# The first rest of each step moved from VectorE to GpSimd in a two-layer recurrence

## The reference

```python
def layer(x, h0, Wx, Wh, b):            # 8 x 1024 x 512, all f32
    xW = einsum('ntd,dh->nth', x, Wx) + b
    def step(h_prev, xw_t):
        h_next = tanh(h_prev @ Wh + xw_t)
        return h_next, h_next
    return scan(step, h0, xW over t)
x = x + layer(x, cond, L0_Wx, L0_Wh, L0_b)
x = x + layer(x, cond, L1_Wx, L1_Wh, L1_b)
```

## Time and profile before

| | us |
|---|---|
| median of 3 runs | 2107.1 (2107.07 to 2107.55) |
| the profiled execution | 2108.6 |
| span from first to last instruction | 2106.8 |
| TensorE busy | 2073.6 |
| VectorE busy | 1720.0 |
| ScalarE busy | 1121.5 |
| GpSimd busy | 14.2 |

### The profile page before, as it was taken

One profiled execution on the slowest core, in us unless ns is written; L12 is line 12 of the kernel. 1 busy time (PEld: TensorE's weight loads), 2 busy tenths in 40 slices (PEclk: granted clock), 3 DMA queues, 4 the chain that ended last, 5 costly groups with the idle time before them and its releaser, 6 DMA issues.

```text
span 2106.8 us, 213809 instructions
## 1 busy us (share of the span) xinstructions
PE 2073.6 (98%) x98432; PEld 1802.2 (86%) x98432; DVE 1720.0 (82%) x10233; ACT 1121.5 (53%) x4609; POOL 14.2 (1%) x15
## 2 busy tenths in 40 slices
PE   7899999999999999999999999999999999999997
PEld 5788888888888888888888888888888888888886
DVE  3788888888888888888888888888888888888886
ACT  2455555555555555555555555555555555555553
POOL 2000000000000000000000000000000000000000
PEclk9999999999999999999999999999999999999999
DMA  3000000000000000000000000000000000000000
GB/s 102 25 23 27 25 25 26 24 27 23 27 23 27 25 24 27 23 27 23 27 24 25 25 24 27 23 27 23 27 24 25 26 24 27 23 27 23 27 25 15
DMA packets 112075, 56.20 MB, mean 27 GB/s; under 512 B 12448, under 2 KB 111024, under 8 KB 111536
## 3 DMA queue, kind: packets, MB, share of 16 engines
q1 hardware_dynamic: 111456, 53.53, 8.9%
q10 hardware_dynamic: 432, 1.18, 0.2%
q0 software_dynamic: 32, 0.02, 0.0%
HBM read 37.90 MB, written 16.78 MB: 26 GB/s over the span
## 4 chain that ended last, share of the span: by engine, by line
PE 98%; issue 1%; DVE 0%; DMA 0%; ACT 0%; SPq 0%; ACTq 0%; DVEq 0%
PE ps_rec L225 43%; PE ps_rec L238 33%; PE ps_xw L206 21%; DMA wx<-wx_in 0%; DVE zt L370 0%; DVE z L376 0%; ACT h L305 0%; SPq L177 0%; SPq L175 0%; ACT ps_rec L300 0%; DVE x_out L420 0%; DVEq L369 0%; ACTq L304 0%; ACTq L299 0%
## 5 line engine op out<-in xcount | busy, mean ns | idle before, releaser
L225 PE MATMUL ps_rec<-wh,h 128*32 128x128 f32 x32896 | 1265.1, 273 | 16.8 <-ACT h L305 12.3
L238 PE MATMUL ps_rec<-wh_part,h 128*32 128x128 bf16 x48960 | 1062.5, 221 | 9.0 <-issue 8.9
L305 ACT ACTIVATE h<-z 128x32 f32<-128x32 f32 x2048 | 470.5, 230 | 846.3 <-DVE z L376 829.5
L225 PEld LDWEIGHTS ps_rec<-wh,h 128*32 128x32 f32 x32896 | 830.3, 109 | 102.6 <-ACT h L305 17.9
L238 PEld LDWEIGHTS ps_rec<-wh_part,h 128*32 128x32 bf16 x48960 | 713.9, 96 | 193.0 <-issue 10.7
L384 DVE TENSOR_TENSOR h<-h 128x16 f32<-128x16 f32 x4080 | 627.2, 154 | 303.0 <-ACT h L305 302.6
L300 ACT ACTIVATE ps_rec<-ps_xw,mask 128x128 f32<-128x128 f32 x2048 | 670.7, 328 | 123.1 <-PE ps_xw L206 97.2
L370 DVE STREAM_TRANSPOSE zt<-ps_rec 128x128 f32<-128x128 f32 x2048 | 638.0, 311 | 39.5 <-PE ps_rec L238 22.3
L376 DVE TENSOR_REDUCE z<-zt 128x32 f32<-128x96 f32 x2048 | 545.9, 267 | 1.5 <-DVE zt L370 0.9
L206 PE MATMUL ps_xw<-wx,x_pe 128*32 128x128 f32 x8192 | 403.1, 273 | 3.3 <-DMA wx<-wx_in 2.4
L206 PE MATMUL ps_xw<-wx,x_mid 128*32 128x128 f32 x8192 | 401.9, 273 | 0.0
(11 more groups left out here) (14 smaller groups left out, 13.5 us busy)
## 6 DMA issues: line engine op xcount, KB each, us to landing
x_pe<-x_t SPq DMA_DIRECT2D x256, 64.0 KB, 1.9
x_dve<-x_t SPq DMA_DIRECT2D x256, 64.0 KB, 2.0
out_t<-x_out SPq DMA_DIRECT2D x256, 64.0 KB, 1.5
wx<-wx_in SPq DMA_DIRECT2D x4, 256.0 KB, 8.2
wh<-wh_in ACTq DMA_DIRECT2D x1, 1024.0 KB, 8.3
wh<-wh_in SPq DMA_DIRECT2D x1, 1024.0 KB, 4.8
wx<-wx_in SPq DMA_DIRECT2D x1, 1024.0 KB, 8.2
bias<-b_in ACTq DMA_DIRECT2D x2, 64.0 KB, 3.3
```

Of the source, the lines that this page charges most:

```text
L225: mm = pe.matmul(rows(bank, g), h_step(l, n - 1)[:, k, :], wh[l][:, k, g * P:(g + 1) * P], start=False, stop=k == KC - 1 and whole.start = ...
L238: mm = pe.matmul(rows(bank, g), h_bits(l, n - 1)[:, k, :], wh_part[l][:, i, at:at + P], start=False, stop=k == whole.start - 1 and i == PA ...
L305: act.activation(h_of(l, n), z[l][n % 2][:, :].rearrange("p (k b) -> p k b", k=KC), ACT.Tanh).then_inc(h_last if (l, n) == (0, T - 1) else ...
```

## The change

`rest` becomes a function of the engine. The first rest of every split step is issued by GpSimd, one after another in the order of the steps, each after the same wait for tanh that VectorE had, and counts up `rest_done` as before. VectorE's list loses its two `rest_first`; its `rest_second` keeps its place and its wait. The rests of layer 1's starting state stay on VectorE. The renaming of a local variable (`rest` to `left`) changes nothing.

```diff
+        def rest(eng, l, n, part):
+
+            step, to, of, tiles = h_step(l, n), h_cols(n, part), h_cols(n, part - 1), slice(0, KB[l])
+            return eng.tensor_tensor(step[:, tiles, to], step[:, tiles, of], h_bits(l, n)[:, tiles, of], ALU.subtract)
...
+            for l, n in ORDER:
+                if is_split(l, n):
+                    pool.wait_ge(*h_count(l, n))
+                    rest(pool, l, n, 1).then_inc(rest_done[l], 1)
...
-            def rest_first(l, n):
-                if is_split(l, n):
-                    dve.wait_ge(*h_count(l, n))
-                    rest(l, n, 1).then_inc(rest_done[l], 1)
-
             def rest_second(l, n):
                 if is_split(l, n):
                     dve.wait_ge(rest_done[l], n + 1 if l else n + 2 - PARTED)
-                    rest(l, n, 2).then_inc(split_count(l, n)[0], 1)
+                    rest(dve, l, n, 2).then_inc(split_count(l, n)[0], 1)
...
                 sums(s)
-                if n0 is not None:
-                    rest_first(0, n0)
                 if n1 is not None:
                     turn(1, n1)
...
                     total(1, n1)
-                    rest_first(1, n1)
```

More of the change, by code:

```diff
@@ L358, in _ @@
                 pool.wait_ge(s_wh[l], DMA)
-                full, rest = wh[l][:, 0:KB[l], :].rearrange("p k d -> p (k d)"), wh_rest[l][:, :]
-                pool.tensor_tensor(rest, full, upper(full), ALU.subtract).then_inc(s_wrest[l], 1)
+                full, left = wh[l][:, 0:KB[l], :].rearrange("p k d -> p (k d)"), wh_rest[l][:, :]
+                pool.tensor_tensor(left, full, upper(full), ALU.subtract).then_inc(s_wrest[l], 1)
                 pool.tensor_copy(wh_part[l][:, 0, :], upper(full)).then_inc(s_wpart[l], 1)
                 pool.wait_ge(s_wrest[l], 1)
-                pool.tensor_copy(wh_part[l][:, 1, :], upper(rest)).then_inc(s_wpart[l], 1)
-                pool.tensor_tensor(wh_part[l][:, 2, :], rest, upper(rest), ALU.subtract).then_inc(s_wpart[l], 1)
+                pool.tensor_copy(wh_part[l][:, 1, :], upper(left)).then_inc(s_wpart[l], 1)
+                pool.tensor_tensor(wh_part[l][:, 2, :], left, upper(left), ALU.subtract).then_inc(s_wpart[l], 1)
+            for l, n in ORDER:
+                if is_split(l, n):
+                    pool.wait_ge(*h_count(l, n))
+                    rest(pool, l, n, 1).then_inc(rest_done[l], 1)
         @block.vector
@@ L466, in _ @@
             dve.wait_ge(s_hinit, 2)
-            rest(1, -1, 1).then_inc(s_hrest, 1)
+            rest(dve, 1, -1, 1).then_inc(s_hrest, 1)
             dve.wait_ge(s_hrest, 1)
-            rest(1, -1, 2).then_inc(s_hsplit, 1)
+            rest(dve, 1, -1, 2).then_inc(s_hsplit, 1)
             for s in range(T + LAG + 1):
```

## The result

The changed kernel takes 2112.3 us (median of 7 runs, 2109.7 to 2114.7) against 2107.1 (also 7 runs, 2105.4 to 2109.0): the ratio is 1.0024, 95% interval 1.0013 to 1.0035. It is slower by 5 us, a little more than the 0.2% that the prediction called the least that can be told. The time lies in the range that was given, but the forecast was "no change", and there is one. The profiled execution took 2111.05 us, its span 2109.3.

A forecast was written before the change was run, and what follows sets the result against it. The prediction took the ring through TensorE to hold half slots at 1.00 us. From 2108.6 us profiled, -1 us for half slots and +0.6 for the last eight steps gave 2108.2, median 2106.7; range 2100 to 2130.

The forecast's parts named there:

- What bounds the kernel: Opening step: two equal rings hold each half slot (one step) at 1.00 us, TensorE's floor just below at 0.99.
- The two rings of 1.00 us: Per half slot: one over VectorE and ScalarE (transpose, reduce, tanh, first rest), one through TensorE; each sums to 1.00 us.
- the floor of 0.99: TensorE's own minimum per half slot; about 0.01 us of each is TensorE waiting for the second rest, counted as busy.
- the ring through TensorE: Transpose, other layer's second rest, L238's split matmuls, next transpose: 1.00 us per half slot, read as the ring that holds.
- Does the transpose stand behind the first rest: Step on VectorE's queue: hold of 0 to 0.01 us per half slot, gain 0 to 20 us, taken as 1 us.
- The first rival: The first rest truly holds the transpose; half slots fall to 0.99, gaining 20 us, 2087 us; chance 0.10.
- GpSimd's cost: First rest on GpSimd: record taken as 0.20 us, between 0.10 and 0.26; waking after tanh 0.04 to 0.08 us.
- The room: From tanh's end to the second rest's start, 0.36 to 0.37 us; less two wakings, 0.25 to 0.29 for GpSimd's record.
- the second rival: GpSimd's record or waking exceeds the cover, deciding from 0.29 us; at 0.32, +41 us, 2147 us; chance 0.15.
- The sign that was named for it: If GpSimd decides: VectorE idle before its second rest, released by GpSimd, and L238's loads show idle time VectorE ends.
- the move at +0.07 in these steps: Last eight steps, layer 1 alone: tanh to second rest grows from 0.23 to 0.28-0.32 us, +0.6 us in all.
- The third rival: GpSimd twice as slow as VectorE, record 0.35 us: half slot 1.05, +102 us, 2208 us; chance 0.05.

The follow-up runs named there:

- The last experiment but one: Changed kernel without first rests, TensorE not waiting for the second rest, which goes to an unread tile: 2085.3 us, ratio 0.9915 to the kernel before.
- the first: Changed kernel with no first rest on any engine, the second rest waiting for tanh itself: 2105.2 us, ratio 0.9994 to the kernel before.
- the second measurement: Changed kernel as it is, measured again on one chip with its last three variants: 2111.5 us against 2103.9 for the kernel before, ratio 1.0039.

## Why the prediction was right or wrong

**What bounds the kernel: right.** The two rings of 1.00 us and the floor of 0.99 under them were read from the rows. The last experiment but one found the floor (19 us, forecast 18 and up to 2 more), and the first showed that the ring through TensorE is enough to hold 1.00 alone.

**Does the transpose stand behind the first rest: right.** The transposes are free in the changed kernel, 494 us of idle time ahead of them, and nothing was gained; without any first rest the gain is 0.0006 of the time, with an interval that includes none. What decided it in the rows was the reduce: the record of a transpose that is queued starts later, but what follows comes at 0.34 in place of 0.35 (in the changed kernel 0.35 again, 1000.58 to 1000.93). The first rival, 20 us, is out.

**GpSimd's cost: the record right, the waking at the edge.** I took 0.20 for the record, and it is 0.212. That is partly luck, as 0.20 was no more than a value picked between 0.10 and 0.26. One row was also misread on the way: the two memsets of 1,096 elements overlap, and each lasts 1.03 us, not half of 1.98. I took 0.04 to 0.08 for the waking, and it is 0.08 (1000.46 to 1000.54). The slow end of my own bounds was the true one.

**The room: this step failed.** The prediction took the room from tanh's end (1001.73) to the start of the second rest's record (1002.10) and subtracted two wakings, which left 0.25 to 0.29 us for GpSimd's record. The start of a record isn't the moment at which its input must be there. A second rest that stands behind a transpose has a record of 0.13, one whose input comes last has one of 0.18 (2095.36 above); both end at the same time if the late one starts 0.04 to 0.05 earlier. The cover is shorter by that: 0.25 less 0.05 is 0.20 us, and GpSimd takes 0.21. In the ring of the second rival, (1.71 + y) / 2, the 1.71 held the short record and the quick waking. With 0.05 and 0.04 added and y = 0.21 it is 2.01 / 2 = 1.005 in place of 0.96. The rival was the right mechanism with its deciding point at y = 0.29 in place of about 0.20, and so it was given 0.15 where it should have been the likeliest. The sign that was named for it, VectorE idle before its second rest and released by GpSimd, would have missed it too: that is 6.0 us in the whole changed kernel.

The number was within reach. The last steps of the kernel before show this very ring bare, with both rests on VectorE. After the tanh at 2093.12 and the reduce at 2094.77 of the earlier trace rows, the timeline of the kernel before goes on with the next tanh, 1.95 after the last:

```profile
2095.07 0.23 ACT L305 ACTIVATE h<-z 128x32 f32<-128x32 f32 x1 [1.49 <-DVE z L376]
```

The prediction itself put the move at +0.07 in these steps, and wrote it down as 0.6 us for eight of them. 1.95 + 0.07 is 2.02, over the 2.00 of two half slots: the same sum, applied to the middle, says slower by up to 0.01 for each half slot, 20 us at most. Measured, the step at the end went from 1.95 to 2.00, 0.05 more, and the middle from just under the limit to just over it.

**The size.** The loss is 5 us over 2,032 half slots (8 in the second measurement), 2.6 to 3.7 ns each. One half slot doesn't show that to 0.01 us, sixteen do, which is one turn of TensorE's loop of 8 slots. In the kernel before it runs from the transpose at 1056.05 of the earlier trace rows to this one:

```profile
1072.10 0.32 DVE L370 STREAM_TRANSPOSE zt<-ps_rec 128x128 f32<-128x128 f32 x1
```

In the changed kernel the same sixteen are these:

```profile
1057.20 0.32 DVE L379 STREAM_TRANSPOSE zt<-ps_rec 128x128 f32<-128x128 f32 x1 [0.42 <-PE ps_rec L243]
...
1073.29 0.32 DVE L379 STREAM_TRANSPOSE zt<-ps_rec 128x128 f32<-128x128 f32 x1 [0.42 <-PE ps_rec L243]
```

16.05 before and 16.09 after: 2.5 ns for each half slot, 5 us in all. It is spread over the steps and not due to a few late ones: the median second rest is 135 ns, against 132 without a first rest, and the longest is 177 in both. Why the lateness settles at 3 to 4 ns isn't shown; the sum of 2.01 above is too coarse for it.

**The third rival**, GpSimd twice as slow as VectorE, is out: 0.212 against 0.175, the mean of VectorE's first rests with the second on GpSimd, is 1.2 times. The rule of "GPSIMD Engine Reference" of the Trainium skill, section 4.1, isn't borne out at 16 elements. The move loses all the same, but by the 0.05 in the ring and not by twice the time.

## What to carry to other kernels

Where a step is moved to another engine and its consumer seems to wait for something else, compare the ends of the consumer's records and not their starts: an instruction queued behind another has a short record, one that waits for its input a long one, and the difference (0.04 to 0.05 us here) comes off the room. Look for a stretch in which the chain runs without cover, such as the steps of one layer alone; its period, compared with the rhythm of the busy stretch, is the slack. And before asking where to move an instruction, leave it out once: here that gave nothing, so no place for it could.

## What the runs showed of the hardware

- GpSimd's tensor_tensor with one f32 and one bf16 input takes 212 ns for 16 elements per partition and 196 for 2. That is 1.1 ns for an element and about 0.19 us fixed; with the 1,887 ns for 1,024 elements it is 1.7 for the others. GpSimd's spans are rough in this profile; that the record's end is meant as it stands is borne out by the second rest, which starts 0.04 after it (2095.32 to 2095.36).
- GpSimd's tensor_tensor starts 0.08 us after the end of the tanh that it waits for (1000.46 to 1000.54), VectorE's 0.04 (1001.73 to 1001.77 in the earlier trace rows).
- A VectorE tensor_tensor of 128x16 lasts 132 ns behind a transpose and about 175 when its input comes last. Lateness up to the difference shows as a longer record with no idle time ahead.
- A two-input subtraction on GpSimd and one on VectorE ran with records that overlap by 0.14 us (1001.67 to 1001.81), with no change in the mean of either beyond 1 ns (154 and 213).
